# Perceiver block on one Trainium2 core: the order of the opening, ahead of the attention's steps

## What is computed

```python
lat = layer_norm(_layernorm(x), g, b)            # 1024 x 256
ctx = layer_norm(context, g, b)                  # 16 x 1024 x 256
q = lat @ Wq                                     # 16 heads of 64
k, v = split(ctx @ Wkv);  k = apply_rope(k, cos, sin)
attn = softmax(clip(q k^T / 8, -11, 11))
x = x + (attn v) @ Wo + bo
x = x + linear_attention(_layernorm(x));  x = x + top2_of_8_experts(_layernorm(x))
```

## Time and profile before

| what | us |
|---|---|
| median of 3 runs | 1332.1 |
| lowest and highest run | 1330.44, 1334.6 |
| the profiled execution | 1325.56 |
| its span | 1323.8 |
| PE busy in the span | 1283.9 |
| DVE, POOL, ACT busy | 891.8, 587.6, 582.4 |

### The profile page before, as it was taken

One profiled execution on the slowest core, in us unless ns is written; L12 is line 12 of the kernel. 1 busy time (PEld: TensorE's weight loads), 2 busy tenths in 40 slices (PEclk: granted clock), 3 DMA queues, 4 the chain that ended last, 5 costly groups with the idle time before them and its releaser, 6 DMA issues.

```text
span 1323.8 us, 43423 instructions
## 1 busy us (share of the span) xinstructions
PE 1283.9 (97%) x18116; PEld 1137.9 (86%) x18116; DVE 891.8 (67%) x1866; ACT 582.4 (44%) x1234; POOL 587.6 (44%) x619
## 2 busy tenths in 40 slices
PE   7799999999999999999999999999999899899996
PEld 3489989889889899898898898998989787789996
DVE  5788777877778777778777787777765366521111
ACT  5244454454444444544544544445444333334332
POOL 3565445555455455455554554554432133222221
PEclk9999999999999999999999999999999999899999
DMA  7143433434343434334343434343454621476663
GB/s 219 35 123 74 119 87 97 122 74 111 86 105 83 114 74 119 85 99 122 75 109 88 105 82 115 74 118 79 105 135 84 211 78 62 144 227 176 191 170 82
DMA packets 71665, 147.61 MB, mean 112 GB/s; under 512 B 17368, under 2 KB 45728, under 8 KB 69280
## 3 DMA queue, kind: packets, MB, share of 16 engines
q1 hardware_dynamic: 67392, 139.71, 40.1%
q0 software_dynamic: 4080, 5.13, 2.5%
HBM read 62.79 MB, written 15.94 MB: 59 GB/s over the span
## 4 chain that ended last, share of the span: by engine, by line
PE 94%; DVE 2%; ACT 1%; issue 1%; POOL 1%; DMA 1%; POOLq 0%; SPq 0%; ACTq 0%; DVEq 0%
PE bank L1136 28%; PE bank L1166 9%; PE bank L1168 9%; PE bank L1167 9%; PE bank L1122 9%; PE bank L1411 6%; PE bank L1424 6%; PE bank L1178 4%; PE bank L1152 2%; PE bank L1143 2%; PE bank L1255 2%; PE bank L1196 2%; PE bank L1280 1%; PE bank L1313 1%; PE bank L1304 1%
## 5 line engine op out<-in xcount | busy, mean ns | idle before, releaser
L445 POOL TENSOR_TENSOR kr<-kr,ksw 128x1024 f32<-128x1024 f32 x128 | 319.2, 2493 | 462.8 <-DVE pr L768 363.8
L1166 PE MATMUL bank<-x_hi,p_hi 128*128 128x258 f32 x1024 | 300.9, 294 | 0.0
L1168 PE MATMUL bank<-x_hi,p_lo 128*128 128x258 f32 x1024 | 288.5, 282 | 0.0
L1167 PE MATMUL bank<-x_lo,p_hi 128*128 128x256 f32 x1024 | 287.8, 281 | 0.0
L1136 PE MATMUL bank<-ct_hi,wk_hi 128*128 128x512 f32 x512 | 213.8, 418 | 0.4 <-DVE ct_lo L796 0.4
L1136 PE MATMUL bank<-ct_hi,wk_lo 128*128 128x512 f32 x512 | 201.3, 393 | 0.0
L1136 PE MATMUL bank<-ct_lo,wk_hi 128*128 128x512 f32 x512 | 200.6, 392 | 0.0
L784 DVE TENSOR_TENSOR kw<-bank,stab 128x1024 f32<-128x1024 f32 x128 | 156.7, 1224 | 62.0 <-PE bank L1136 62.0
L1167 PEld LDWEIGHTS bank<-x_lo,p_hi 128*128 128x128 f32 x1024 | 194.7, 190 | 0.0
L1168 PEld LDWEIGHTS bank<-x_hi,p_lo 128*128 128x128 f32 x1024 | 193.6, 189 | 0.0
L1166 PEld LDWEIGHTS bank<-x_hi,p_hi 128*128 128x128 f32 x1024 | 193.2, 189 | 0.0
(11 more groups left out here) (189 smaller groups left out, 1920.6 us busy)
## 6 DMA issues: line engine op xcount, KB each, us to landing
ksw<-kw SPq DMA_DIRECT2D x512, 128.0 KB
raw<-in_ctx_dram SPq DMA_DIRECT2D x16, 1024.0 KB, 6.1
w_two<-in_L_ffn_W_dram SPq DMA_DIRECT2D x16, 1024.0 KB, 4.9
x_slots<-fill SPq DMA_DIRECT2D x128, 64.5 KB, 3.3
w_all<-in_L_ffn_W_dram SPq DMA_DIRECT2D x4, 2048.0 KB, 15.2
wo<-in_L_ffn_W_dram SPq DMA_DIRECT2D x7, 1024.0 KB, 5.1
xs<-x_slots SPq DMA_DIRECT2D x23, 129.0 KB, 2.3
raw<-in_x_dram SPq DMA_DIRECT2D x4, 512.0 KB, 4.3
```

What stands on the lines that cost most here:

```text
L445: pool.tensor_tensor(kr[:, i], kr[:, i], ksw[:, i], ALU.add).then_inc(kr_done, 1)
L1166: pe.matmul(psZ[:, 0:D + 2], p_hi[:, i, c], x_hi[:, b, t], start=(t == 0), stop=False, skip_group_check=True)
L1167: pe.matmul(psZ[:, 0:D], p_hi[:, i, c], x_lo[:, b, t], start=False, stop=False, skip_group_check=True)
L1168: last = pe.matmul(psZ[:, 0:D + 2], p_lo[:, i, c], x_hi[:, b, t], start=False, stop=(t == ST - 1), skip_group_check=True)
```

## The change

It reorders the opening and alters nothing behind step -1.

- DVE takes the statistics of all eight tiles of context batch 0 in one run, ahead of the first xhat, into the arrays of the latents (xl_mom); POOL makes their roots in two instructions of four columns (xl_rsd). The steps do statistics and roots only from tile 8 on.
- ACT writes wk_hi right behind the first four latent turns and DVE wk_lo right behind the first xhat. Before they stood behind queries 5 and 6 on ACT and in steps -6 and -5 on DVE.
- The first four latent turns go through eight banks, one for each half tile. ACT writes the first half of latT, DVE the second (new semaphore latT_dve).
- T0 stands behind queries(1, 0), where it stood behind queries(2, 0), and so on; T7 comes ahead of queries(1, 1).
- POOL fills feat_w, cvec and vbd at its start and the other constants ahead of step -12.
- vec2_ps, vec2_done, early_ps and total_ps give way to further counts of vec_ps, vec_done and count_ps.

```diff
+        def lat_bank(t, k):
+            return bank[:, ((7, 6, 5, 4), (0, 1, 2, 3))[k][t] if t < TT // 2 else 7 - t % 2, k * P:(k + 1) * P]
@@ POOL
             pool.wait_ge(consts_done, 1)
+            pool.memset(feat_w[:], 0.0).then_inc(feat_w_zero, 1)
...
+            pool.memset(vbd[:], 0.0).then_inc(vbd_zero, 1)
...
-                if there(j + 12):
+                if ST <= j + 12 and there(j + 12):
...
+            for c in range(2):
+                t = slice(c * ST // 2, (c + 1) * ST // 2)
+                pool.wait_ge(stats_done, (c + 1) * ST // 2)
+                pool.tensor_tensor(xl_vpe[:, t], xl_mom[:, t, 1], consts[:, 3:4].to_broadcast([P, ST // 2]), ALU.add).then_inc(var_done, ST // 2)
+                pool.wait_ge(var_done, (c + 1) * ST // 2)
+                pool.tensor_tensor(xl_rsd[:, t], xl_vpe[:, t], consts[:, 2:3].to_broadcast([P, ST // 2]), ALU.pow).then_inc(rstd_done, ST // 2)
+            constants()
             for j in range(-12, 0):
                 step(j)
-                if j == -4:
-                    constants()
@@ ACT
-                for k in range(KC):
-                    last = act.activation(latT[:, k, t * P:(t + 1) * P], bank[:, 6 + t % 2, k * P:(k + 1) * P], ACT.Identity,
+                for k in range(1 if t < TT // 2 else KC):
+                    last = act.activation(latT[:, k, t * P:(t + 1) * P], lat_bank(t, k), ACT.Identity,
...
             for t in range(TT // 2):
                 lat_turned(t)
+            key_weights(0)
+            key_weights(1)
             for g in range(PAIRS):
                 queries(g, 0)
                 if g < TT // 2:
                     lat_turned(TT // 2 + g)
-                if g in (5, 6):
-                    key_weights(g - 5)
-                if g >= 2:
-                    step(g - 12)
+                if g >= 1:
+                    step(g - 11)
             queries(0, 1)
-            step(-4)
             step(-3)
@@ DVE
+                if t == TT // 2 - 1:
+                    dve.wait_ge(vec_done, 1)
+                    for u in range(TT // 2):
+                        dve.wait_ge(latT_ps, u + 1)
+                        dve.tensor_scalar(latT[:, 1, u * P:(u + 1) * P], lat_bank(u, 1), vecs[:, 0, 1:2], vecs[:, 1, 1:2], ALU.mult, ALU.add).then_inc(latT_dve, 1)
...
+            dve.wait_ge(ctx_ld[0], 16)
+            for t in range(ST):
+                dve.bn_stats(xl_st6[:, t], raw[:, 0, t]).then_inc(bn_done, 1)
+                dve.wait_ge(bn_done, t + 1)
+                dve.bn_aggr(xl_mom[:, t], xl_st6[:, t]).then_inc(stats_done, 1)
             dve.wait_ge(affine_ld, 32)
-            step(-12)
             step(-11)
...
+            key_weights(0)
+            key_weights(1)
+            for j in range(-10, -2):
                 step(j)
-                if j in (-6, -5):
-                    key_weights(j + 6)
@@ PE, turn_lat
+                if t == 0:
+                    pe.wait_ge(tab_done, 2)
+                    pe.wait_ge(vec_done, 1)
+                if t >= TT // 2:
+                    pe.wait_ge(latT_done, (1, 2, 5, 6)[t - TT // 2])
...
-                if g >= 2:
-                    step(g - 12)
+                if g >= 1:
+                    step(g - 11)
             queries(0, 1)
-            step(-4)
+            step(-3)
             queries(1, 1)
-            step(-3)
             queries(2, 1)
```

More of the change, by code:

```diff
@@ L426, in _ @@
             pool.wait_ge(consts_done, 1)
+            pool.memset(feat_w[:], 0.0).then_inc(feat_w_zero, 1)
+            pool.memset(cvec[:, 0:1], -0.5)
+            pool.memset(cvec[:, 1:2], EPS)
+            pool.memset(vbd[:], 0.0).then_inc(vbd_zero, 1)
+            pool.wait_ge(vbd_zero, 1)
+            for b in range(2):
+                at = b * (AD + 1) + AD
+                pool.memset(vbd[b * N:(b + 1) * N, :, :, at:at + 1], 1.0).then_inc(vbd_ones, 1)
+                pool.wait_ge(vbd_ones, b + 1)
             for c in range(2):
@@ L457, in constants @@
             def constants():
[L458 to L466, removed]
                 pool.memset(square[:], 1.0).then_inc(mask_done, 1)
@@ L621, in late_turns @@
                 if j == STEPS - 10:
-                    act.wait_ge(vec2_ps, 1)
-                    act.copy(vecs2[:], psT[:, 0:E * FT + 4]).then_inc(vec2_done, 1)
+                    act.wait_ge(vec_ps, 2)
+                    act.copy(vecs2[:], psT[:, 0:E * FT + 4]).then_inc(vec_done, 1)
                 if j in (STEPS - 9, STEPS - 8):
@@ L636, in _ @@
                     turned(0)
-            act.wait_ge(vec2_done, 1)
+            act.wait_ge(vec_done, 2)
             def keys_queries(t):
@@ L759, in step @@
                     b, t = place(j + 11)
-                    i = (j + 11) % 2
                     wait(dve, rstd_done, j + 12)
-                    dve.scalar_tensor_tensor(out=raw[:, b, t], in0=raw[:, b, t], scalar=mv[:, i, 0:1], in1=ctx_scale[:],
+                    dve.scalar_tensor_tensor(out=raw[:, b, t], in0=raw[:, b, t], scalar=moments_of(j + 11)[0], in1=ctx_scale[:],
                                              op0=ALU.subtract, op1=ALU.mult).then_inc(scaled, 1)
@@ L770, in step @@
                     b, t = place(j + 11)
-                    i = (j + 11) % 2
                     wait(dve, scaled, j + 12)
-                    dve.scalar_tensor_tensor(out=raw[:, b, t], in0=raw[:, b, t], scalar=rstd[:, i:i + 1], in1=ctx_shift[:],
+                    dve.scalar_tensor_tensor(out=raw[:, b, t], in0=raw[:, b, t], scalar=moments_of(j + 11)[1], in1=ctx_shift[:],
                                              op0=ALU.mult, op1=ALU.add).then_inc(xhat_done, 1)
-                if there(j + 12):
+                if ST <= j + 12 and there(j + 12):
                     b, t = place(j + 12)
@@ L1103, in turn_lat @@
                 pe.wait_ge(xl_norm, t + 1)
-                if t >= 2:
-                    pe.wait_ge(latT_done, t - 1)
+                if t == 0:
[3 more added lines that the diff above has]
+                    pe.wait_ge(latT_done, (1, 2, 5, 6)[t - TT // 2])
                 for k in range(KC):
-                    last = pe.transpose(bank[:, 6 + t % 2, k * P:(k + 1) * P], xl[:, t, k * P:(k + 1) * P], ident[:])
+                    last = pe.transpose(lat_bank(t, k), xl[:, t, k * P:(k + 1) * P], ident[:])
                 last.then_inc(latT_ps, 1)
@@ L1185, in queries @@
                     if c == 0:
+                        pe.wait_ge(latT_dve, TT // 2)
                         pe.wait_ge(tab_done, 2)
@@ L1293, in features @@
                 if t == 0:
-                    pe.wait_ge(vec2_done, 1)
+                    pe.wait_ge(vec_done, 2)
                     pe.wait_ge(exp_done, STEPS)
@@ L1387, in _ @@
                     pe.wait_ge(prefix_done, EARLY_TILES)
-                    pe.matmul(bank[:, 4, 0:E], ones[:], before[:, EARLY_TILES], start=True, stop=True).then_inc(early_ps, 1)
+                    pe.matmul(bank[:, 4, 0:E], ones[:], before[:, EARLY_TILES], start=True, stop=True).then_inc(count_ps, 1)
                 if s + 2 < TT:
@@ L1444, in _ @@
             pe.wait_ge(prefix_done, TT)
-            pe.matmul(bank[:, 7, E:2 * E], ones[:], before[:, TT], start=True, stop=True).then_inc(total_ps, 1)
+            pe.matmul(bank[:, 7, E:2 * E], ones[:], before[:, TT], start=True, stop=True).then_inc(count_ps, 1)
             rank(TT - 1)
```

18 lines of the change are left out of this document (9 added, 9 removed).

## The result

| | before | changed |
|---|---|---|
| median of 6 runs each, us | 1330.21 | 1321.67 |
| lowest and highest | 1326.2, 1334.6 | 1319.91, 1324.32 |
| ratio of the runs, 95% interval | 1 | 0.9948, 0.9929 to 0.9967 |
| the profiled execution | 1325.56 | 1323.79 |
| its span | 1323.8 | 1322.1 |

The profiled executions differ by 1.8 us only, the medians by 8.5, the starts of S0 by 5.85. Which of the three is the change's worth is the first thing to settle.

A forecast was written before the change was run, and what follows sets the result against it. TensorE, 97% busy, bounds the kernel. First key projection: 13.05 + 23.3 + 1.1 + 1.55 + 0.2 + 0.45 = 39.65, 5.1 us earlier; taken off the 1332.1 median, 1327.0 us, range 1323.8 to 1330.5.

The forecast's parts named there:

- q0 at 13.05: First query projection on PE: starts at 13.05 instead of 14.56 through the eight banks, 1.5 us sooner.
- the feat_w copies issued by 42: SP's queue: with the fills moved, the 16 small copies end at 42.3; the sign was issue before 43.
- T0, "+1.1": First context turn: PE arrives at 18.65 and waits to 19.75 for DVE's statistics and normalisation, 1.1 us.
- T1, "+1.55": Second context turn: PE arrives at 21.9 and waits to 23.45 for DVE, delayed by wk_lo, 1.55 us.
- T3, "+0.2": Fourth context turn: 0.2 us allowed because ACT has a last latent turn in that round.
- One doubled pass, +0.45: DVE's first context normalisation beside POOL's second root: one of two passes doubles, 0.45 us.
- 23.3 in the sum: PE's work without waits from first query projection to first key projection: query projections and transposes, 23.3 us.
- S0 could not start before 58.4: First scores, were the fills left in place: held to 58.4 by the exchange of halves, losing 3.2 us.
- T0 and T1 did not grow: Rival: DVE's chain to the second context turn grows 1.1 to 3.1 us more; 1328 to 1330, chance 0.13.
- the exchange did not bound S0: Rival: the exchange of halves sets the first scores' start; gain 2.0 us, 1330.1, chance 0.04.
- the end followed: Rival claimed the opposite: later waits take the opening's gain, so the time stays at 1332; chance 0.05.
- the clock did rise: Rival claimed the opposite: PE stays at 1.2 GHz in the opening, 11.5 us later, 1343.6; chance 0.04.

The follow-up runs named there:

- the second comparison: The unaltered changed kernel timed once more against the kernel before: median 1322.13 against 1327.77 us, ratio 0.9957.
- the quarters: Changed kernel with DVE's wk_lo in four 128x512 pieces, one after tile 0's pass, three in later steps; run twice, ratios to before 0.9944 and 0.9939.

## Why the prediction was right and wrong

**Right.** The bound and the mechanism: waits ahead of K0, made by DVE's round trips to POOL, which go, and a gain that reaches the end whole. q0 at 13.05, where the hundredth is luck: it lay between 12.90 and 13.33 in nine profiles with the eight banks. Right too: both waits at T0 and T1 made by DVE, none over 0.3 us from T4 to K0; the feat_w copies issued by 42; no wait for POOL at S0. The range of the gain, 4 to 7 us, holds the 5.85 of S0 and the 0.9957 of the second comparison.

**Wrong: the number that the gain was taken from.** "The median of the runs shown is 1332.1 ...; I take the same 5.1 off". That median was of three runs, of a program whose next medians were 1327.3, 1327.6 and 1327.8. The prediction named the sign of it, the profiled execution 0.5% below the median, and drew nothing from it. 5.1 us from 1327.5 is 1322.4, and the changed kernel's medians were 1321.67 and 1322.13. Of the miss of 5.3 us 4.6 are this; the other 0.7 are of the size of the gain's own miss (5.85 and not 5.1).

For the profiled execution I had forecast 1320.5, and it took 1323.79, a miss the other way: its rest behind step 126 took 314.3 us where that of before took 310.2. The sum has no term for this scatter. The second execution of the changed kernel took 1321.99.

**Wrong by size: the waits at T0 and T1**, 3.3 us in the sum with T3 and the neighbour on the port; they were 2.1.
- T0, "+1.1": 0.4 by the starts (18.95 to 19.33). DVE's pieces of latT ended 0.2 sooner and its statistics came at 0.53 each, so x0 was ready at 19.3, not 19.65; and PE came 0.3 later, as its turn of latent tile 4 took 0.42 us and not 0.22. I had priced it by a row at the high clock.
- T1, "+1.55": 1.5 by the starts (21.54 to 23.08).
- T3, "+0.2": 0.2 (27.20 to 27.41).
- "One doubled pass, +0.45": 0. The passes took 0.47 and 0.48 beside POOL, and POOL paid instead, its addition 0.30 where the first took 0.20 and its root 1.19 where the first took 1.01. Both passes (18.29, 18.79) began ahead of POOL's instruction (18.52, 18.96). Here the Trainium skill (SBUF — State Buffer, section "SBUF: two separate sides") says that whoever starts first holds the pair and the other waits. The trace agrees for these two, and not in all: wk_lo began at 19.29, while the root was under way to 20.15, and took 1.23 us, where in the kernel before it took 1.21 and 1.22; and in the kernel before the pass that began 0.03 us ahead of x_lo paid all the same. The sum should have asked who comes first; where the starts lie within 0.05 us, the rows don't say who pays.

PE's own work from q0 to K0, 23.3 in the sum, took some 23.7, 0.3 of it ahead of T0 as said. In all K0 came at 38.9 (13.05 + 23.7 + 2.1) and not at 39.65, and S0 at 54.5 and not at 55.3, which makes the 5.85 of 5.1. DVE's pieces of latT took 0.38 each and not 0.3, which cost nothing, as ACT's ended last.

**Wrong in a part: the fills.** "S0 could not start before 58.4 and 3.2 us of my gain would go": they would cost nothing (S0 54.33). A step of the old order was kept at its old time, though the change moves the step it hangs on. **Not priced apart: the early key weights.** The sum charged their cost at T1 and counted what they save among the waits that vanish; putting them back shows 1.3 to 1.4 us net. Nor do the eight banks give 1.5 us by themselves: 0.7 to 0.9.

The rivals: T0 and T1 did not grow, the exchange did not bound S0, the end followed, and the clock did rise. Its moment moves S0: in the two profiles of the quarters, with q1 at 2.59 and 1.72 us, S0 came 40.65 and 40.19 us behind q0.

## What to carry to other kernels

Where the middle of a program is bound by one engine, judge an edit of its opening by when the first bound instruction starts: here that point repeats within 0.25 us for one kernel (in one run, where a pass of DVE and one of POOL started 0.02 us further apart, it moved by 0.5), while the whole time scatters by 4 to 8 and a pair of profiled executions showed 1.8 us of a gain of 5.85. Before a forecast in absolute time, look whether the profiled execution and the median of the few runs agree. When pricing "without this part", move everything that hangs on the new order first.

## What the runs showed of the hardware

- The clock's rise is not tied to the first unbroken work. With q0 at 12.9 to 13.3 in nine profiles, q1 took from start to start 1.72 us in four of them, 1.88 and 1.91 in two and 2.24, 2.49 and 2.59 in three. So a lead ahead of the rise is partly lost: of the 1.5 us of the eight banks alone 0.7 were left at S0.
- A DVE pass of 128x256 and POOL's x_lo that start 0.03 to 0.05 us apart: one of the two takes 0.3 to 0.5 us longer. It was DVE's pass with 0.03 and 0.04 us of lead (0.95, 0.96), and POOL's with 0.05 (0.93 and not 0.64).
- The granted clock between 1015 and 1050 us was 1.00, 0.95 or 0.90 in different executions, and the rest of the span behind step 126 309.6 to 311.1, 311.2 to 314.3 and 314.9 to 315.9 us. These 6 us are of the size of the runs' scatter (4 to 8 us), and no edit of the opening is shown to cause it.
